# A perceiver kernel's selective scan: decays in PSUM, step inputs on GpSimd, context work in the units without broadcasts

## What is computed

```python
delta = softplus(delta @ dt_w.T + dt_b)              # one step size per token and channel
dA = jnp.exp(jnp.einsum('bld,dn->lbdn', delta, A))   # decays, 16 states per channel
dBu = jnp.einsum('bld,bln,bdl->lbdn', delta, B, u)   # inputs
carry = a * carry + bu                               # over the 256 tokens of each sequence
y = jnp.einsum('bdn,bn->bd', carry, c)               # products with C, summed over the states
y = y + u * D[:, None];  y = y * silu(res)
```

## Time and profile before

| | |
|---|---|
| median of 3 runs | 2045.66 us (2039.83 to 2051.41) |
| the profiled execution | 2051.5 us, first to last instruction |
| TensorE busy in it | 1795.8 us (88%) |
| DVE busy | 1518.3 us (74%) |
| ScalarE busy | 1205.8 us (59%) |
| GpSimd busy | 234.1 us (11%) |
| first scan of unit 0 to the end of the loop | 405.58 to 781 us of the span |

### The profile page before, as it was taken

One profiled execution on the slowest core, in us unless ns is written; L12 is line 12 of the kernel. 1 busy time (PEld: TensorE's weight loads), 2 busy tenths in 40 slices (PEclk: granted clock), 3 DMA queues, 4 the chain that ended last, 5 costly groups with the idle time before them and its releaser, 6 DMA issues. The chain is left out here.

```text
span 2051.5 us, 32916 instructions
## 1 busy us (share of the span) xinstructions
PE 1795.8 (88%) x12549; PEld 1222.8 (60%) x12549; DVE 1518.3 (74%) x1768; ACT 1205.8 (59%) x2132; POOL 234.1 (11%) x243
## 2 busy tenths in 40 slices
PE   7989998878888885799998799999999999996754
PEld 5877785456655663678787455555555555554523
DVE  6546553469988995565655689999998999983565
ACT  1333332587667762443534188888887888892463
POOL 4223301000000000222322000010010000000000
PEclk8999998999999997899999899999999999998977
DMA  9798842147755662121213956557566646510000
GB/s 360 265 326 317 316 160 88 65 163 255 249 203 206 227 242 81 62 68 65 67 44 65 147 129 128 100 112 126 114 106 109 128 98 120 95 26 12 1 0 21
DMA packets 172012, 280.32 MB, mean 137 GB/s; under 512 B 21568, under 2 KB 100672, under 8 KB 164688
## 3 DMA queue, kind: packets, MB, share of 16 engines
q1 hardware_dynamic: 170128, 277.72, 48.2%
q10 hardware_dynamic: 1728, 0.49, 0.2%
HBM read 187.50 MB, written 88.15 MB: 134 GB/s over the span
## 5 line engine op out<-in xcount | busy, mean ns | idle before, releaser
L2193 DVE TENSOR_REDUCE xn_peaks<-psum 128x2 f32<-128x1024 f32 x512 | 621.4, 1224 | 42.7 <-PE psum L2019 34.9
L2148 ACT ACTIVATE moe_mix_transposed<-psum 128x512 f32<-128x512 f32 x1024 | 552.8, 597 | 71.9 <-PE psum L2024 20.7
L2024 PE MATMUL psum<-xn_q_stack,xn_k_words 50*128 50x256 f32 x2048 | 377.2, 307 | 12.8 <-DVE xn_peaks L2193 6.3
L2024 PEld LDWEIGHTS psum<-xn_q_stack,xn_k_words 50*128 50x128 f32 x2048 | 249.8, 186 | 214.5 <-ACT moe_mix_transposed L2148 185.9
L2019 PE MATMUL psum<-xn_k_words,xn_q_stack 50*128 50x512 f32 x1024 | 371.8, 450 | 5.9 <-DMA xn_q_stack<-q_rows 3.8
L2056 PE MATMUL psum<-moe_mix_transposed,xn_v 128*32 128x256 f32 x4096 | 328.8, 393 | 2.0 <-issue 0.3
L2019 PEld LDWEIGHTS psum<-xn_k_words,xn_q_stack 50*128 50x128 f32 x1024 | 185.4, 185 | 14.2 <-DVE xn_peaks L2193 7.4
L1133 DVE TENSOR_TENSOR_SCAN mx_state<-mx_decay,mx_state 128x1024 f32<-128x1024 f32 x64 | 151.5, 2367 | 4.2 <-POOL mx_decay L858 4.2
L321 PE MATMUL psum<-xw_ctx_natural,xw_weights_transposed 128*128 128x256 f32 x512 | 124.8, 389 | 13.3 <-DVE xw_weights_transposed L473 13.1
L2056 PEld LDWEIGHTS psum<-moe_mix_transposed,xn_v 128*32 128x32 f32 x4096 | 81.8, 108 | 73.7 <-issue 8.3
L723 ACT ACTIVATE ctx_k_words<-psum,ctx_bk 128x512 fp32r<-128x512 f32 x128 | 86.6, 684 | 57.0 <-PE psum L153 35.2
(11 more groups left out here) (318 smaller groups left out, 2576.2 us busy)
## 6 DMA issues: line engine op xcount, KB each, us to landing
xn_k_words<-k_words SPq DMA_DIRECT2D x384, 128.0 KB, 6.7
...
k_words<-ctx_k_words SPq DMA_DIRECT2D x128, 256.0 KB, 2.4
...
```

Of the source, the lines that this page charges most:

```text
L2024: return pe.matmul(PS[:, narrow_bank("exp", n, step, a), half * S:(half + 1) * S], K[n % XN_KSLOTS][narrow_rows(a), kt * P:(kt + 1) * P], ...
L2148: act.activation(t["weights"][:, step % 4, a, :, :], bank.rearrange("p (t s) -> p t s", t=2), ACT.Exp, scale=XN_SCALE).then_inc(s.taken, 1)
L2193: dve.tensor_reduce(t["peaks"][:, m % 2, q, :, c], PS[:, 2 * (x % 2):2 * (x % 2) + 2, :], AX.X, ALU.max).then_inc(s.top_read, 1)
```

## The change

- The decays go to PSUM, banks 0 to 3: two slots (`MX_DECAYS`) instead of three. ScalarE writes 255 of each 256 cells; the cells where a sequence begins are zeroed once by DVE before the loop, and GpSimd's 64 small memsets are gone.
- GpSimd makes the inputs du x B (64 products of 128 x 1,024), one unit ahead; du itself moves to DVE (`changes`). A product for unit i waits until DVE has multiplied unit i - 3 with C and added unit i - 4.
- DVE multiplies with C one unit after the scan (`MX_MUL`), adds two units after it, TensorE sums four units after it (`MX_SUM`), in one bank (4) for all groups. There are 6 state slots instead of 5.
- Spreads use banks 6 and 7, and context parts rotate through banks 5, 6 and 7 (`ctx_bank`). As both need 6 and 7, `mx_context` has no step in broadcast units: steps 5 to 68 lie in the 24 plain units of the first half, 69 to 128 in the 24 of the second, 2.67 and 2.5 per unit.

```diff
-MX_DECAYS, MX_STATES, MX_AHEAD, MX_BEHIND = 3, 5, 2, 2
+MX_DECAYS, MX_STATES = 2, 6
+MX_MUL, MX_ADD, MX_SUM = 1, 2, 4
+MX_EARLY, MX_PAUSED = 4, 68
+def ctx_bank(i, part):
+    return CTX_BANK + (4 * i + part) % CTX_BANKS      # 5 + ... % 3
 # context_pe: what keys and values wait for
-            pe.wait_ge(kr[m], 2 * i)
+        if i and m == 0:
+            pe.wait_ge(kr[1], 2 * i)
+        elif i:
+            pe.wait_ge(s.vc, 2 * i - 1)
...
-            pe.wait_ge(s.vc, 2 * i - 1 + pair)
+        if pair:
+            pe.wait_ge(kr[0], 2 * i + 2)
+        elif i:
+            pe.wait_ge(s.vc, 2 * i)
-def mx_context(point):
-    return MX_EARLY - (-(CTX_STEPS - MX_EARLY) * point // (2 * MX_UNITS))
+def mx_context(new, part):
+    half, m, q = mx_unit(new)
+    whole = MX_EARLY, MX_PAUSED, CTX_STEPS
+    span = 2 * (MX_DT - 1) * MX_NU
+    done = 2 * ((m - 1) * MX_NU + q) + part + 1 if m else 0
+    return whole[half] - (-(whole[half + 1] - whole[half]) * done // span)
+    t["decay"] = [k.PS[:, MX_NQ * i:MX_NQ * (i + 1), :] for i in range(MX_DECAYS)]
+def mx_sums(new):
+    late = new - MX_SUM - 1
+    now = new - MX_SUM
+    return [i for i in (late,) if i >= MX_NU and i % MX_NU == 0] + [
+        i for i in (now,) if 0 <= i < MX_UNITS and (i == 0 or i % MX_NU)]
 # mixer_pool
-        pool.memset(starts, 0.0).then_inc(s.start, 1)
+        if i >= 1 + MX_ADD:
+            pool.wait_ge(s.cmul, i - MX_ADD)
+        if i >= 2 + MX_ADD and mx_added(i - MX_ADD - 2):
+            pool.wait_ge(s.cadd, (i - MX_ADD - 1) // 2)
+        pool.tensor_tensor(t["state"][:, i % MX_STATES, :, :],
+                           t["du"][:, m % 2, None, :].to_broadcast([P, MX_NQ, MX_HALF]),
+                           t["Bb"][:, q * MX_NQ:(q + 1) * MX_NQ, :], ALU.mult).then_inc(s.bin, 1)
 # mixer_pe, the loop
+    for new in range(MX_UNITS + MX_SUM):
+        if new < MX_UNITS:
+            if m == 0:
+                spread(half, q)
+            ctx.upto(mx_context(new, 0))
+        for i in mx_sums(new):
+            total(i)
+        if new < MX_UNITS:
+            ctx.upto(mx_context(new, 1))
 # mixer_dve
+    dve.memset(PS[:, 0:MX_DECAYS * MX_NQ, :].rearrange("p n (b s) -> p n b s", b=2)[:, :, :, 0], 0.0).then_inc(s.starts, 1)
+    def changes(c):
...
+        dve.tensor_tensor(t["du"][:, m % 2, :], t["delta"][:, m, tokens], t["U"][:, m, tokens], ALU.mult).then_inc(s.du, 1)
 # mixer_dve, the loop
+        if i < MX_UNITS:
+            recur(i)
+        if 0 <= i - MX_MUL < MX_UNITS:
+            outputs(i - MX_MUL)
+        if 0 <= i - MX_ADD < MX_UNITS and mx_added(i - MX_ADD):
+            added(i - MX_ADD)
```

More of the change, by code:

```diff
@@ L579 @@
 CTX_STEPS = 4 * CTX_CHUNKS
+CTX_BANK, CTX_BANKS = 5, 3
 def context_scratch(k):
@@ L680, in keys @@
         wait_chunk(pe, s, i)
-        products(k, PS[:, banks[m], :], [[t["wk2"][:, a, kd, m * P:(m + 1) * P] for a in range(2)] for kd in range(KD)],
+        products(k, PS[:, ctx_bank(i, m), :], [[t["wk2"][:, a, kd, m * P:(m + 1) * P] for a in range(2)] for kd in range(KD)],
                  [[t["words"][:, i % 2, a, kd, :] for a in range(2)] for kd in range(KD)]).then_inc(kp[m], 1)
@@ L712, in context_pe, with context_act @@
     return Steps(step)
-def context_act(k, t, sems, banks):
+def context_act(k, t, sems):
     s, kp, kr, ks = sems
@@ L822, in mixer_sems @@
     return k.sems("mx", "clear in_w small proj out_w inproj xc tap u gate xproj xdbl word_hi word_lo aexp a "
-                        "delta_pe z size dexp w ln rest less delta spread_pe spread du dec start bin scan cmul cadd "
+                        "delta_pe z size dexp w ln rest less delta spread_pe spread du starts dec bin scan cmul cadd "
                         "sum y g out x", clear)
@@ L897, in step_sizes @@
             pe.wait_ge(s.xdbl, 1)
-            pe.wait_ge(s.gate, 7)
+            pe.wait_ge(cs[0].vc, 2)
         elif c == 1:
@@ L914, in spread @@
                 pe.wait_ge(s.spread, r - 1)
-            pe.matmul(PS[:, r % 2, :], t["pick"][:, row:row + 1].to_broadcast([P, P]),
+            if half and q == 0 and j == 0:
+                pe.wait_ge(cs[0].vc, MX_PAUSED // 2)
+            pe.matmul(PS[:, MX_SPREAD + r % 2, :], t["pick"][:, row:row + 1].to_broadcast([P, P]),
                       t["xwords"][:, half * MX_HALF:(half + 1) * MX_HALF], start=True, stop=True).then_inc(s.spread_pe, 1)
@@ L924, in total @@
         if q == 0:
-            if group >= 2:
-                pe.wait_ge(s.y, group - 1)
+            if group:
+                pe.wait_ge(s.y, group)
             else:
@@ L930, in total @@
         for j in range(parts):
-            last = pe.matmul(PS[:, 4 + group % 2, :], k.ident[:], t["state"][:, i % MX_STATES, j, :],
+            last = pe.matmul(PS[:, MX_Y, :], k.ident[:], t["state"][:, i % MX_STATES, j, :],
                              start=(q + j == 0), stop=(q == MX_NU - 1 and j == parts - 1))
@@ L936, in mixer_pe @@
         step_sizes(c)
-    for i in range(-MX_AHEAD, MX_UNITS + MX_BEHIND):
-        new = i + MX_AHEAD
-        ctx.upto(mx_context(2 * new + 1))
-        if new < MX_UNITS and mx_unit(new)[1] == 0:
-            spread(mx_unit(new)[0], mx_unit(new)[2])
-        for c in MX_LATER.get(new, ()):
-            step_sizes(c)
-        if 0 <= i < MX_UNITS:
-            ctx.upto(mx_context(2 * new + 2))
-        if i >= MX_BEHIND:
-            total(i - MX_BEHIND)
+    for new in range(MX_UNITS + MX_SUM):
+        if new < MX_UNITS:
+            half, m, q = mx_unit(new)
+            if m == 0:
+                spread(half, q)
+            elif m == 1 and q == 0:
+                pe.wait_ge(s.spread, 2 * MX_N * (half + 1))
+            for c in MX_LATER.get(new, ()):
+                step_sizes(c)
+            ctx.upto(mx_context(new, 0))
[3 more added lines that the diff above has]
+            ctx.upto(mx_context(new, 1))
     pe.wait_ge(s.out_w, 16)
@@ L952, in mixer_pe @@
         if tile < 2:
-            pe.wait_ge(s.spread, 2 * 2 * MX_N - 1 + tile)
+            pe.wait_ge(s.scan, MX_UNITS)
         else:
@@ L1157, in gated @@
         dve.scalar_tensor_tensor(t["U"][:, m, tokens], t["U"][:, m, tokens], t["skip"][:, m:m + 1],
-                                 PS[:, 4 + group % 2, :], ALU.mult, ALU.add).then_inc(s.y, 1)
+                                 PS[:, MX_Y, :], ALU.mult, ALU.add).then_inc(s.y, 1)
         dve.wait_ge(s.y, group + 1)
         dve.tensor_tensor(t["U"][:, m, tokens], t["U"][:, m, tokens], t["gate"][m][:, tokens], ALU.mult).then_inc(s.g, 1)
-    inputs(0)
-    for i in range(MX_UNITS + MX_BEHIND):
+    for i in range(MX_UNITS + MX_SUM):
         if i < MX_UNITS:
             recur(i)
-        elif i == MX_UNITS and mx_added(i - 1):
-            added(i - 1)
-        if i >= MX_BEHIND and (i - MX_BEHIND) % MX_NU == MX_NU - 1:
-            gated(i - MX_BEHIND)
+        if 0 <= i - MX_MUL < MX_UNITS:
+            outputs(i - MX_MUL)
+        if 0 <= i - MX_ADD < MX_UNITS and mx_added(i - MX_ADD):
+            added(i - MX_ADD)
+        if mx_chunk(i, 7):
+            remainder(mx_chunk(i, 7))
+        if mx_chunk(i, 4):
+            softplus(mx_chunk(i, 4))
+            changes(mx_chunk(i, 4))
+        if i >= MX_SUM and (i - MX_SUM) % MX_NU == MX_NU - 1:
+            gated(i - MX_SUM)
     for tile in range(NT):
```

100 lines of the change are left out of this document (44 added, 56 removed).

## The result

The changed kernel takes 2074.36 us (median of 4 runs, 2072.54 to 2075.06) against 2048.30 (4 runs, 2039.83 to 2051.41): 1.0116 times as long, 95% interval 1.0078 to 1.0155. It is slower, as forecast, by 26 us where 15 were forecast. In the profiled executions the loop, from the first scan to the first residual addition, takes 410.8 us (398.85 to 809.67) where it took 378.8 (405.58 to 784.40); what lies around the loop moved by some us in both directions.

What follows compares the result with a forecast made beforehand. DVE was taken to pace the plain units, TensorE's context work close behind. Loop: 76.5 + 297.1 + 11 + 5 + 1 = 390.6 us against 375.4, 15 us longer; on the median 2045.66 that gives 2061 us, range 2032 to 2086.

Steps and rivals of the forecast that it cites:

- The signs it named: Profile after: scans 2.3 us, DVE 75% or less in plain units, R's waits near 0.8 us in about 42 places.
- Broadcast units, 76.5 us: 16 units without context steps, paced by DVE at 4.1 us each plus group operations: 76.5 us against 114.8.
- seven operations on 512 columns; at 0.65 each: DVE's softplus, du and gate, once a group of eight units: 4.6 us.
- slow-clock rival: Broadcast units: TensorE at 1.2 GHz makes a unit take 5.1 us, 16 us more, 2077 us; chance 0.10.
- Plain units, 297.1 us: 48 units with 31 context chunks on TensorE: 254.8 for chunks, 61.2 for 72 T, less 18.9; 9.6 us a chunk.
- less 18.9: Plain units: credit for T (TensorE's state sums) filling idle time between K and R, 10 x 0.85 + 10 x 1.04.
- the sum has 1 us: Loop's end: the last unit passes product, addition and sum four units later, 1 us.
- Logarithms and clock, 11 + 5 us: Plain units: five logarithms at 2 us plus 1 for the shorter softplus step; TensorE's slow clock 5, between 0 and 12.
- some 13 us at the low level: Plain units before the change: TensorE's time at the 1.2 GHz clock, about half of it taken as cost.
- DVE's relief: DVE drops the product with B and zeroed-cell waits: 4.1 us a unit, 37.4 us per eight broadcast units with group operations.
- The lock rival: Scan also waits for GpSimd, or GpSimd for it: loop 443 us, 68 us more, 2114 us; chance 0.07.
- The relief rival: Context chunks keep pace, loop ends with DVE: at 8.7 us a chunk 17 us less, 2028 us; chance 0.18.

Runs made afterwards that it cites:

- Run 1: Kernel before, with only its context steps planned as in the changed kernel (none in broadcast units): 2069.3 us, 1.0102 times the kernel before.
- run 2: Changed kernel with all 124 context steps placed before the loop's first unit: 2255.5 us, one run.
- run 11: Changed kernel with softplus's logarithm replaced by an absolute value, so no function table changes: 2056.1 us, 1.0046 times the kernel before.
- run 3: Kernel before with all context steps placed before the loop's first unit: 2263.0 us, one run.
- run 5: Changed kernel with the inputs (product with B) made by DVE again, GpSimd idle in the loop: 2076.2 us, 1.0127 times the kernel before.
- run 6: Changed kernel with odd units' decays in SBUF, even units' still in PSUM: 2083.4 us, 1.0149 times the kernel before.
- Run 9: Kernel before with only a chunk's product order changed, V between each K and its R: 2035.9 us, 0.9947 times the kernel before.

## Why the prediction was right, and where it was off

- **The direction and the mechanism** held. The prediction said that 38 us are gained where TensorE idles and 53 lost where the whole context work is packed; measured are 28 and 63. Run 1 shows that the plan does this: 25 of the loop's 32 us come with the plan alone. The signs it named are there: scans of 2.3 us, DVE at 71% in the plain units, R's waits of 0.78 us in most of 43 places.
- **Broadcast units, 76.5 us; measured 86.7.** The mis-sized term is "seven operations on 512 columns; at 0.65 each". The prediction held the product with C for subject to the lock, and forgot that the gate and softplus have two SBUF inputs as well: in run 2 three of them take 7.8 us in place of 2.1, in the second broadcast group here two of them take 5.1. That group's products with C take 1666 ns in the mean. The rest went to waiting: in the first group DVE is busy for only 37.0 of 44.7 us, and TensorE's granted clock there is 0.77, at the 1.2 GHz level from 411 to 421 and from 431 to 438 us. So the slow-clock rival is present in part; how much of the 10 us it holds was not separated.
- **Plain units, 297.1 us: right by the chunk, too small for the stretch.** R has no wait in any of the 17 places in the plain units where T stands right before it (20 were forecast), as in this chunk of the changed kernel:

```profile
718.90 1.55 PE L153 MATMUL psum<-ctx_chunk_words,ctx_wk_words 128*128 128x512 f32 x6
720.29 1.02 PE L958 MATMUL psum<-mx_state,identity 128*128 128x512 f32 x2
721.23 0.50 PE L694 MATMUL psum<-ctx_k_words,ctx_minus_identity 128*128 128x512 f32 x1
721.57 1.56 PE L153 MATMUL psum<-ctx_chunk_words,ctx_wk_words 128*128 128x512 f32 x6
723.91 0.50 PE L694 MATMUL psum<-ctx_k_words,ctx_minus_identity 128*128 128x512 f32 x1 [0.78 <-ACT ctx_k_words L733]
724.25 3.04 PE L153 MATMUL psum<-ctx_wv_words,ctx_chunk_words 128*128 128x256 f32 x24
727.13 1.54 PE L153 MATMUL psum<-ctx_chunk_words,ctx_wk_words 128*128 128x512 f32 x6
```

  From K to R it is 2.33 us with T between (721.23 - 718.90) and 2.34 without, and the chunk takes 8.23 us. The 23 chunks that lie whole in the plain units and meet no logarithm took 221.2 us together. The prediction's prices give 217.5 for them with its credit for T in R's waits, 229.9 without, so "less 18.9" was a sound step. But the plain units take 306.6 us even in run 11, without logarithms. What was sized too small lies at least in part at the ends of the stretches, for which the sum has 1 us: in the changed kernel the last V of the first half ends 6.2 us before the scan of unit 32 (603.23 against 609.41), and the last of the second 9.2 us before the loop's end (800.52 against 809.67), filled in part by sums. No run separates these ends. That the sum without the credit, 254.8 + 61.2 = 316.0, comes near run 1's 315.7 is chance, as run 1 has its logarithms too.
- **Logarithms and clock, 11 + 5 us.** Measured together by run 11: 17.5 us in the plain units, of which R's waits are 11.2. Right in size, with luck in the parts. R's waits behind four logarithms were 4.15, 3.63, 4.10 and 4.52 us rather than 1 to 3, and behind the fifth (table load at 525.39 us) there was none. The "some 13 us at the low level" is the first plain stretch alone: by the earlier trace rows both have about 23 us, and half of that would have been 12, not 5.
- **DVE's relief.** In eight units with the group's own operations it was priced at 5.5 us (42.9 before, 37.4 forecast) and is 2.4 (40.50 against 42.89, runs 2 and 3); in the whole kernel run 5 finds no more than 1.9. The gain in the broadcast units comes mostly from the missing context work (run 1: 26.7 us with no relief at all), and not from the 4.1 us a unit at which the prediction priced DVE.
- **The lock rival** falls for the scan (64 of 64 at most 2.29 us), and run 6 shows what it would have cost with decays in SBUF in half the units: 8.8 us of the loop, in one trace each (the intervals of the two ratios overlap).
- **The relief rival** falls: its break-even is a chunk of 9.1 us in the mean, and the 23 above have 9.6, with the four at logarithms 10.5. But the prediction also said that a chunk under 9.1 us would make it wrong, and five came under it, with 8.22 to 8.59 us, where no more than one T stands. A single chunk was the wrong sign; the mean decides.
- **The bound before.** The prediction took DVE as the pace in the plain units and TensorE as a close second. Run 9 shows that TensorE's chain bound the broadcast units and part of the rest: the kernel gets 0.5% faster by the order of its products alone, with DVE's work unchanged.
- **The total** came out 13 us over the forecast. The loop was 20 us over (410.2 against 390.6). That the total is nearer is luck: the stages around the loop, which the change does not touch, took 10 us less in this trace than in the one before (the mixer's first product starts at 338.23 us against 344.56; in five other traces it starts between 338.28 and 344.58).
